# The query-side causal mask of the first attention: matmuls on TensorE replaced by an add inside VectorE's maximum

## The reference, cut to what matters

```python
scores = jnp.einsum('bqhd,bkhd->bhqk', q, k) / math.sqrt(Hd)
causal = jnp.triu(jnp.ones((S, S), dtype=bool), k=1)
scores = jnp.where(causal, jnp.finfo(scores.dtype).min, scores)
attn = jax.nn.softmax(scores, axis=-1)
out = jnp.einsum('bhqk,bkhd->bhqd', attn, v)
...
x = x + attention_A(xn) + graph_B(xn)
```

## Time and profile before

| | us |
|---|---|
| time, median of 3 runs | 1459.75 (1459.38 to 1459.88) |
| the profiled execution's own time | 1460.57 |
| its span, first to last instruction | 1458.8 |
| PE busy | 1407.9 (97%) |
| DVE busy | 1185.3 (81%) |
| ACT busy | 1167.2 (80%) |
| POOL busy | 445.5 (31%) |

### The profile page before, as it was taken

The page is one execution under the profiler, slowest core; times in us unless marked ns, Lnnn a source line. Parts: engine busy times, 40 slices in busy tenths (PEclk is TensorE's granted clock), DMA queues, the critical chain, the costliest instruction groups (busy, mean ns, idle before and its releaser), DMA issues.

```text
span 1458.8 us, 62514 instructions
## 1 busy us (share of the span) xinstructions
PE 1407.9 (97%) x27498; PEld 859.0 (59%) x27498; DVE 1185.3 (81%) x1207; ACT 1167.2 (80%) x2219; POOL 445.5 (31%) x930
## 2 busy tenths in 40 slices
PE   6899999999999999999999999999999999999993
PEld 4568887755556555655565555655555655556641
DVE  8778887798888878888788787887888878889772
ACT  3378887788888878888788888887888888888791
POOL 5231113334322332333323332233323342231110
PEclk9899999999999999999999999999999999999996
DMA  7131112344232332233323323242233322331211
GB/s 247 41 119 50 56 53 81 121 127 142 71 108 94 117 104 70 98 104 103 106 76 120 104 68 125 77 127 97 74 104 106 109 97 83 101 105 61 62 43 50
DMA packets 116080, 138.53 MB, mean 95 GB/s; under 512 B 14945, under 2 KB 90466, under 8 KB 115682
## 3 DMA queue, kind: packets, MB, share of 16 engines
q1 hardware_dynamic: 115810, 134.54, 28.2%
HBM read 65.04 MB, written 62.39 MB: 87 GB/s over the span
## 4 chain that ended last, share of the span: by engine, by line
PE 87%; DMA 4%; DVE 3%; SPq 2%; ACT 2%; POOL 1%; issue 1%; ACTq 0%; DVEq 0%; POOLq 0%
PE s L963 53%; PE cps L1058 25%; PE misc L963 7%; DMA qs<-mrows 1%; ACT probs L744 1%; DMA dram_raw_b<-csb 1%; DVE neg_max L920 1%; SPq L418 1%; PE misc L958 1%; DMA ctx_b<-dram_raw_b 0%; DVE fin L827 0%; DMA ks<-dram_qk_a 0%; DMA ks<-dram_qk_b 0%; SPq L450 0%; POOL parts L568 0%
## 5 line engine op out<-in xcount | busy, mean ns | idle before, releaser
L920 DVE TENSOR_REDUCE neg_max<-s 128x1 f32<-128x1024 f32 (+7 forms) x1024 | 1121.4, 1106 | 230.9 <-PE s L963 167.8
L744 ACT ACTIVATE probs<-s 128x512 f32<-128x512 f32 x1792 | 1051.7, 600 | 217.4 <-PE s L963 171.3
L963 PE MATMUL s<-qs,ks 99*32 99x512 bf16 (+2 forms) x7680 | 762.9, 370 | 8.4 <-DMA qs<-mrows 3.1
L963 PE MATMUL s<-ks,qs 96*32 96x512 bf16 (+2 forms) x7680 | 590.1, 370 | 6.9 <-DMA ks<-dram_qk_a 4.7
L1058 PE MATMUL cps<-probs,vs 128*32 128x256 f32 (+1 forms) x7552 | 567.3, 368 | 0.3 <-ACT probs L744 0.3
L963 PEld LDWEIGHTS s<-qs,ks 99*32 99x32 bf16 x7680 | 226.1, 94 | 260.9 <-ACT probs L744 116.8
L1058 PEld LDWEIGHTS cps<-probs,vs 128*32 128x32 f32 x7552 | 272.3, 110 | 119.1 <-issue 16.8
L963 PEld LDWEIGHTS s<-ks,qs 96*32 96x32 bf16 x7680 | 246.7, 98 | 113.4 <-issue 17.2
L600 POOL TENSOR_TENSOR mparts<-neg_max,zeros 128x8 bf16<-128x8 f32 x128 | 25.8, 201 | 779.4 <-DVE neg_max L920 779.4
L666 POOL TENSOR_TENSOR parts<-full,zeros 128x512 bf16<-128x512 f32 x48 | 61.3, 1278 | 82.2 <-ACT full L775 82.2
L963 PE MATMUL misc<-srcT,cur 128*32 128x512 f32 x544 | 71.7, 592 | 0.0
(11 more groups left out here) (122 smaller groups left out, 575.6 us busy)
## 6 DMA issues: line engine op xcount, KB each, us to landing
dram_qk_b<-parts SPq DMA_DIRECT2D x48, 384.0 KB, 3.3
qs<-dram_qk_b SPq DMA_DIRECT2D x96, 192.0 KB
ks<-dram_qk_b SPq DMA_DIRECT2D x96, 192.0 KB
dram_qk_b<-parts SPq DMA_DIRECT2D x48, 256.0 KB, 3.1
dram_raw_b<-csb SPq DMA_DIRECT2D x96, 128.0 KB, 4.3
dram_qk_b<-parts SPq DMA_DIRECT2D x48, 128.0 KB, 3.1
vsrc<-srcT SPq DMA_DIRECT2D x12, 512.0 KB, 3.1
ctx_b<-dram_raw_b SPq DMA_DIRECT2D x48, 128.0 KB
```

The costliest lines, as they stand in the source:

```text
L744: nc.scalar.activation(buf[:, lo:hi], s2[bank][:, 0:hi - lo], ACT.Exp, scale=scale).then_inc(exp_done, 1)
L920: last = ve.tensor_reduce(neg_max[k % 2][:, t:t + 1], s1[n % 2][:, lo:hi], AX.X, ALU.max, negate=True)
L963: last = te.matmul(dst[c0:c0 + STRIP, :], lhsT[:, c0:c0 + STRIP], rhs, start=start, stop=stop, tile_position=(0, c0))
```

## The change

The mask of the query-major scores of A is no longer added on PE. `mask_q` becomes an fp32 tile as wide as `s1` (1024 columns), zero except for the triangle in its last 128 columns. DVE's `tensor_reduce` becomes, in A only, a `tensor_tensor_reduce`: it adds the scores of a tile to the last columns of `mask_q`, multiplies by -1, writes the result over the scores in PSUM, and takes the minimum of it into `neg_max`. B keeps `tensor_reduce`, and the key-major mask keeps its matmuls. DVE waits once, at the start, for POOL's constants.

```diff
-        mask_q = sb("mask_q", [128, 128], BF16)
+        mask_q = sb("mask_q", [128, S])
...
-            pl.affine_select(out=mask_q[:, :], in_=mask_q[:, :], pattern=[[-1, 128]], compare_op=ALU.is_ge,
-                             fill=MASKED, base=0, channel_multiplier=1).then_inc(pool_const, 1)
+            pl.affine_select(out=mask_q[:, S - 128:S], in_=mask_q[:, S - 128:S], pattern=[[-1, 128]],
+                             compare_op=ALU.is_ge, fill=MASKED, base=0, channel_multiplier=1).then_inc(pool_const, 1)
...
+            dve.wait_ge(pool_const, N_CONST)
             dve.wait_ge(wb_in, 16 * 11)
...
                             for t, lo, hi in query_tiles(kind[0], i):
-                                last = ve.tensor_reduce(neg_max[k % 2][:, t:t + 1], s1[n % 2][:, lo:hi], AX.X,
-                                                        ALU.max, negate=True)
+                                scores, peak = s1[n % 2][:, lo:hi], neg_max[k % 2][:, t:t + 1]
+                                if kind[0] == "A":
+                                    last = ve.tensor_tensor_reduce(
+                                        out=scores, in0=scores, in1=mask_q[:, S - hi + lo:S], scale=-1.0,
+                                        scalar=-MASKED, op0=ALU.add, op1=ALU.min, accum_out=peak)
+                                else:
+                                    last = ve.tensor_reduce(peak, scores, AX.X, ALU.max, negate=True)
                             last.then_inc(max_done, 1)
...
-                                    diagonal = kind[0] == "A" and hi == end
                                     last = mm_strips(s1[n % 2][:, lo:hi], q[0:KROW, t * 128:(t + 1) * 128],
-                                              ky[0:KROW, lo - at:hi - at], stop=not diagonal)
-                                    if diagonal:
-                                        last = mm_strips(s1[n % 2][:, end - 128:end], ident_h[:, :], mask_q[:, :],
-                                                  start=False)
+                                              ky[0:KROW, lo - at:hi - at])
```

## The result

The changed kernel takes 1450.03 us (median of 6 runs, 1448.12 to 1450.51) against 1459.82 for the kernel before; ratio 0.9926, 95% interval 0.9915 to 0.9937. That is 9.8 us or 0.7% faster. The profiled execution took 1450.35 us with a span of 1448.5, against 1460.57 and 1458.8: 10.3 us less span.

The account below looks back on a forecast made before the run. PE was taken to bound A, with DVE nearly level after the change. AL -5.4, AZ -3.1, A0 -2.6 and +0.7 for its first steady unit sum to -10.4 us, from 1459.75 to 1449.3; range 1446 to 1468.

Parts of the forecast that it names:

- The bound: In A, PE sets the pace: 6.91 us a unit of AL without a gap, DVE busy for 5.75.
- the mask group's own row is a trap: Mask matmuls on PE: 59.8 us busy, but 0.055 us a group between starts, so A gives back 14.1 us at most.
- x: Extra DVE time per masked reduction in A, eight a unit: taken as 0.09 us, with ends 0 and 0.23.
- DVE is now level with PE: In AL, DVE's load brings the unit to 6.57 us, against PE's 6.47; gain 5.4 us over 16 units.
- my own formula: Total change as a function of x: -22.7 + 136x us while DVE bounds AL (from x = 0.08), zero at 0.167.
- the very first unit: First unit of A0, filled by biases and loads: no gain counted.
- rival 1: In AL and A0, DVE becomes the bound at x = 0.20: +10 us, 1470; chance 0.20.
- A0's first steady unit: DVE works there without a gap and PE already waits 0.50 us for it: loses 8x = 0.7 us.
- The costs counted as nothing: At the start: POOL's larger `mask_q` fill, about 1 us more, and DVE's wait for constants, both covered; up to 1 us otherwise.
- Rival 4: In A, DVE's in-place PSUM write makes each column take two cycles: about +136 us, 1596; chance 0.03.
- Rival 3: In A, the minimum comes free, x = 0 to 0.05: AL gains 7.0 us, total -12.7, 1447; chance 0.12.

Follow-up runs that it names:

- the DVE half alone: Against the kernel before: DVE masks as in the changed kernel, while PE still adds the mask by matmuls with operands exchanged; ratio 1.0006.
- The kernel with three copies: Changed kernel with three one-column DVE copies ahead of each masked reduction of A; ratio 1.0019 to the kernel before.
- the PE half alone: Against the kernel before: query-major mask matmuls removed, DVE keeps tensor_reduce, so the query-side mask is left out of the maximum; ratio 0.9932.

## Why the prediction was right

**The bound.** That PE bounds A and that the mask group's own row is a trap held: of 59.8 us busy 13 us at most could be gained. A group measured 0.051 us, not 0.055, so AL could give 6.5 us, not 7.0. The two halves confirm it from both sides for AL.

**The mis-sized term is x.** I took 0.09 from start-to-start costs of other instructions; it is 0.037 to 0.051 by busy time and 0.029 under load with copies between. What failed is the step from those rows to the new one. The masked reduction does have a second instruction, as the Trainium skill, VectorE: DVE Perf Modes, stated in the section named above, but my sentence that by it x would be at least a small instruction's start-to-start cost, 0.070, is refuted: the read starts together with the next main instruction, and that one is only 39 to 51 ns longer than the old reduction. What that section states holds in this trace; what I drew from it doesn't. Hence "DVE is now level with PE" was wrong: 0.41 us of idle time are left before a unit's first turn, PE doesn't wait for `neg_max` in AL, and AL gained 6.5, not 5.4.

**Why the sum still fitted.** With x = 0.037 my own formula gives -12.4: AL -7.0, AZ -3.1, A0 -2.6 and +0.3. The measured span change is -10.3, so other errors took 2.1 us of it back. In AL the smaller mask group took 0.5. In AZ it was 0.5: only four of its eight units run at 7.78 us, not all as I had it; the second one, 6.91 before, now waits for keys and loses 0.13. In A0 the last unit gains 0.07 instead of 0.44, with PE waiting 1.77 us for the keys' transfer where it waited 1.42, and five others gain a little under 0.44 each, 0.25 together. The waits in A0 and AZ:

```profile
107.40 0.61 PE L969 MATMUL s<-ks,qs 96*32 96x512 bf16 x8 [1.77 <-DMA ks<-dram_qk_a]
224.96 0.62 PE L969 MATMUL s<-ks,qs 96*32 96x512 bf16 x8 [0.37 <-DMA ks<-dram_qk_a]
```

The start and B each are 0.6 longer. Neither is shown to be the edit's: in three profiled executions of the changed kernel itself the first unit starts at 39.55 to 40.47 us and B takes 1177.2 to 1179.4, and over all kernels here, with the same B, it goes from 1175.5 to 1180.2. Against all that, the very first unit, which I had counted at nothing, gained 0.7 in this pair. That eight masks cost twice as much at half clock would give as much, but it isn't shown: with all masks still there, the DVE half alone had a first unit of 9.68 us instead of 11.21, at full clock from 46 us on, where the others were still at half. The forecast's number is right partly because these errors cancel, which is luck; that A gains and PE holds the gain is not.

**A price that was inconsistent.** At x = 0.20 the prediction's formula gives +4.5 us, its rival 1 +10, since the rival gives AZ a smaller gain and lets A0 lose. The kernel with three copies, x = 0.17, lies between: its AZ and A0 gain 1.3 and 0.2 us, where the formula gives 3.1 and 1.3.

**A0's first steady unit** lost 0.34 us (7.51 to 7.85), 8 x 0.043: the place was right, at half the price. Of the six after it, five gained 0.36 to 0.42, the last 0.07. **The costs counted as nothing** were nothing: `mask_q`'s fill takes 0.95 us on POOL, ahead of 5.8 us of idle time, and DVE's products start at 27.85 us, no later than before.

**The rivals.** Rival 1's mechanism exists: the kernel with three more copies has it, and the sign has turned there, near the x that was worked out. Rival 4 is out: 1232 ns for 1024 columns. Rival 3 had the right bound in AL, PE, and about the right x, though the minimum doesn't come out in one instruction; I gave it 0.12 as I had let a sentence of the Trainium skill stand for a price. Its number, -12.7, is further off than the forecast's.

## What to carry to other kernels

Price a group that runs in strips beside others by the distance between starts, not by its busy time, and work out first how much the relieved and the loaded engine each need per unit of work: the gain is the difference to the next bound, here hand-overs of ACT and probably POOL, only 0.07 us a unit further on. Where an operation is unknown, work the sum out as a function of its one price and find the zero; for AL that function held when the price did not. And test a result by its halves: the DVE half alone and the PE half alone say in two runs who pays and who gains. When an instruction's price is taken from its row, compare the row at the head of a queue with those that follow one another: here 8 ns and 50.

## What the runs showed of the hardware that I had not expected

- The masked reduction of a fp32 PSUM tile with an fp32 SBUF tile takes 1232 ns for 1024 columns at the head of a turn, against 1224 of the old reduction. Behind another masked reduction it is 39 to 51 ns longer than the old one (332 ns against 281 for 128 columns), and with a small copy between, or with the result in SBUF, that is gone (288 and 286 ns).
- The accumulator's read has a row of 142 ns when the main result goes to PSUM and 83 ns when it goes to SBUF, and starts with the next instruction in both; under load the PSUM write costs 0.018 us an instruction.
- A small DVE instruction ahead of a masked reduction takes 0.07 us from its start to the reduction's, but adds only 0.02 us net when it is one and 0.045 each when they are three.
- PE's granted clock fell to half at different stretches from one execution of the same kernel to the next, which is worth 3.2 us between two profiled executions here, as much as a third of the change.
